# A 27-pass loop on five engines written out in a straight line

## The reference

```python
x = layernorm(x + attention(x))        # 16 query heads, 4 key/value heads of 64, rotary, ALiBi, out @ Wo
x = layernorm(x + cross_attention(x, ctx, cell))   # 16 heads of 16, windows of 64 keys and the 64 before,
                                       # causal, and only where cell[q] == cell[k]; layer norms before q, k, v, o
x = layernorm(x + ffn(x))              # bitlinear: ternary weights, activations rounded to 8 bits;
                                       # down(silu(gate(x)) * up(x)), inner width 1024
```

## Time and profile before

| | |
|---|---|
| median of 3 runs | 2457.42 us (2453.6 to 2459.31) |
| the profiled execution | 2455.23 us |
| its span, first to last instruction | 2453.3 us |
| mean granted TensorE clock | 0.978 |
| instructions | 61,410 |
| DMA | 72.93 MB, 30 GB/s over the span |

### The profile page before, as it was taken

One profiled execution on the slowest core, in us unless ns is written; L12 is line 12 of the kernel. 1 busy time (PEld: TensorE's weight loads), 2 busy tenths in 40 slices (PEclk: granted clock), 3 DMA queues, 4 the chain that ended last, 5 costly groups with the idle time before them and its releaser, 6 DMA issues. The chain is left out here.

```text
span 2453.3 us, 61410 instructions
## 1 busy us (share of the span) xinstructions
PE 2287.2 (93%) x17706; PEld 1662.5 (68%) x17706; DVE 1866.3 (76%) x8005; ACT 1568.6 (64%) x4577; POOL 1219.1 (50%) x1422
## 2 busy tenths in 40 slices
PE   5889999999999999999999999999999999999985
PEld 4666777776677776677766677676667776667652
DVE  4868887777787777787777787777787777787865
ACT  2567766667666667666667666667666667766651
POOL 3445554545554545454555454555455555454521
PEclk8999999999999999999999999999999999999996
DMA  4010110010110010011010011011011011010100
GB/s 156 15 37 20 32 34 19 24 33 24 31 33 25 19 33 27 28 33 32 11 33 27 28 33 32 11 33 30 26 31 32 11 33 30 26 31 24 29 10 13
DMA packets 84569, 72.93 MB, mean 30 GB/s; under 512 B 18336, under 2 KB 79136, under 8 KB 84384
## 3 DMA queue, kind: packets, MB, share of 16 engines
q1 hardware_dynamic: 84384, 71.19, 10.4%
HBM read 45.98 MB, written 8.39 MB: 22 GB/s over the span
## 5 line engine op out<-in xcount | busy, mean ns | idle before, releaser
L1151 POOL TENSOR_TENSOR prob<-prob,precs 128x512 f32<-128x512 f32 x512 | 528.7, 1045 | 414.9 <-DVE precs L809 410.5
L1066 ACT ACTIVATE prob<-prob,nmax 128x256 f32<-128x256 f32 x1024 | 508.3, 499 | 231.8 <-DVE nmax L802 231.8
L802 DVE CUSTOM_DVE_ANT_0 prob<-bank,alibi 128x256 f32<-128x256 f32 x1024 | 372.0, 419 | 148.3 <-PE bank L536 147.4
L1073 ACT COPY pT<-bank 128x512 f32<-128x512 f32 x512 | 298.9, 584 | 287.1 <-PE bank L441 281.2
L1089 ACT ACTIVATE px<-px,nmx 128x128 f32<-128x128 f32 x1024 | 316.0, 390 | 141.8 <-DVE nmx L894 139.8
L441 PE MATMUL bank<-ident,prob 128*128 128x128 f32 x2048 | 320.1, 280 | 8.2 <-ACT pT L1073 7.0
L1142 POOL TENSOR_TENSOR qtok<-qtok,by_sin 128x512 f32<-128x512 f32 x128 | 163.0, 1274 | 297.4 <-DVE by_sin L792 297.3
L441 PEld LDWEIGHTS bank<-ident,prob 128*128 128x128 f32 x2048 | 243.4, 143 | 96.1 <-issue 55.7
L536 PE MATMUL bank<-kk,qq 64*128 64x256 f32 x2048 | 291.3, 403 | 0.9 <-DVE nmax L802 0.9
L554 PE MATMUL bank<-pT,v_sb 128*64 128x256 f32 x2048 | 277.5, 392 | 7.7 <-ACT oT L1078 7.0
L894 DVE CUSTOM_DVE_ANT_0 px<-bank,mask 128x128 f32<-128x128 f32 x1024 | 230.4, 286 | 18.2 <-issue 4.8
(11 more groups left out here) (187 smaller groups left out, 4471.5 us busy)
## 6 DMA issues: line engine op xcount, KB each, us to landing
ctxt<-in_ctx SPq DMA_DIRECT2D x32, 256.0 KB, 2.7
xT<-in_xT SPq DMA_DIRECT2D x32, 256.0 KB, 3.0
cT<-in_ctxT SPq DMA_DIRECT2D x32, 256.0 KB, 2.6
xtok<-in_x SPq DMA_DIRECT2D x32, 256.0 KB, 3.0
kx<-kxT SPq DMA_DIRECT2D x256, 32.0 KB, 2.0
vs<-vx SPq DMA_DIRECT2D x64, 128.0 KB, 2.4
out_y<-y SPq DMA_DIRECT2D x32, 256.0 KB, 2.1
cellk<-in_cell SPq DMA_DIRECT2D x32, 64.0 KB, 2.9
```

Of the source, the lines that this page charges most:

```text
L802: v.tensor_tensor_reduce(out=prob[:, (2 * p + q) % SLOTS, c, :], in0=psum[SCORES[c]][:, q * L:(q + 1) * L], in1=alibi[:, p % 2, c, :], sca ...
L1066: nc.scalar.activation(prob[:, (2 * p + q) % SLOTS, c, :], prob[:, (2 * p + q) % SLOTS, c, :], ACT.Exp, bias=nmax[:, i:i + 1], scale=-1.0, ...
L1073: nc.scalar.copy(pT[:, p % 2, :, :, q * P:(q + 1) * P].rearrange("p c k n -> p (c k) n"), bank[:].rearrange("p (c n) -> p c n", c=4)).then ...
L1151: g.tensor_tensor(prob[:, n % SLOTS, :, :], prob[:, n % SLOTS, :, :], precs[:, 2 * n:2 * n + 2].unsqueeze(2).to_broadcast([P, 2, L]), ALU. ...
```

## The change

For each of the five engines the hardware loop is replaced by a loop of the program that writes the kernel, so that the 27 passes of BODY stand one after the other. The index is then a number, every wait compares with a constant, and every DMA has a constant address. HEAD, BODY, TAIL and `run` are as before. One of the five places, the others are alike (`pe`, `dve`, `act`, `pool` in place of `sp`):

```diff
             run(HEAD)
-            with sp.Fori(0, LAST - FILL) as j:
-                run(BODY, j + FILL)
+            for it in range(FILL, LAST):
+                run(BODY, it)
             run(TAIL)
```

More of the change, by code:

```diff
@@ L687, in _ @@
             run(HEAD)
-            with pe.Fori(0, LAST - FILL) as j:
-                run(BODY, j + FILL)
+            for it in range(FILL, LAST):
+                run(BODY, it)
             run(TAIL)
@@ L1029, in _ @@
             run(HEAD)
-            with dve.Fori(0, LAST - FILL) as j:
-                run(BODY, j + FILL)
+            for it in range(FILL, LAST):
+                run(BODY, it)
             run(TAIL)
@@ L1113, in _ @@
             run(HEAD)
-            with act.Fori(0, LAST - FILL) as j:
-                run(BODY, j + FILL)
+            for it in range(FILL, LAST):
+                run(BODY, it)
             run(TAIL)
@@ L1227, in _ @@
             run(HEAD)
-            with pool.Fori(0, LAST - FILL) as j:
-                run(BODY, j + FILL)
+            for it in range(FILL, LAST):
+                run(BODY, it)
             run(TAIL)
```

## The result

The changed kernel takes 2368.99 us (median of 4 runs, 2367.9 to 2370.26) against 2455.51 us for the kernel before in the same comparison. The ratio is 0.9649, 95% interval 0.9629 to 0.9668: 3.5% faster. The forecast was 2377 us, range 2362 to 2400.

The account below looks back on a forecast made before the run. TensorE was taken to bound the kernel, waiting for oT after VectorE's branch stalls. The wait's 58.8 us and the clock's 19.5, checked by 80.6 from whole passes, were taken as 80 saved, other terms nothing: 2377 us, range 2362 to 2400.

Parts of the forecast that it names:

- The bound and the place: TensorE waits for oT after VectorE's two stalls behind each taken branch: 58.8 us in 26 waits.
- The inference that the packets are VectorE's: Five 8 KB instruction blocks fetched again each loop pass were taken as VectorE's, which alone had an unexplained stall.
- The comparison of whole passes: 26 loop passes against the first, which has no branch before it: 1908.4 - 26 x 70.30 = 80.6 us saved.
- The other sum of the forecast: TensorE's wait for oT, 58.8 us, plus the clock's 19.5 us: together 78.3 us.
- The clock: TensorE's granted clock falls after the gap in about every second pass; 19.5 us, about 14 passes of 1.4 us.
- Rival (a): Gap goes, but the clock still falls or half a microsecond of wait returns each pass: about 2397 us, chance 0.08.
- The registers: Removing register operations in the 27 passes saves between nothing and 21 us; taken as nothing.
- Rival (b): Register work lay behind the last idle 0.77 us a pass; another 17 to 21 us go: about 2358, chance 0.04.
- TensorE's fetches: Straight code brings new 16 KB instruction blocks each pass, at most 1.6 us a block; taken as nothing.
- Rival (c): TensorE stalls at its instruction blocks: 2593 us at 1.6 us each, slower from 0.6 us a block; chance 0.05.
- Rival (d): No effect: VectorE's loop stays resident, packets are another engine's, the stall belongs to the step: 2457 us, chance 0.03.

Follow-up runs that it names:

- the kernel with 30: Kernel before, all loops kept, 30 semaphore increments added to VectorE ahead of HEAD: 2367.03 us, ratio 0.9628; timed again 2367.31 us.
- the kernel with 80: Kernel before, all loops kept, 80 semaphore increments added to VectorE ahead of HEAD: 2396.93 us, ratio 0.9755.
- 128: Kernel before, all loops kept, 128 semaphore increments (one whole block) added to VectorE ahead of HEAD: 2454.48 us, ratio 0.9983.

## Why the prediction was right, and where it was off

**The bound and the place.** The forecast named TensorE's wait for oT, made by VectorE's stalls behind the branch, and that was right. The wait went with VectorE's loop and with nothing else, in number (26, 8, 2 waits for 26, 8, 2 branches), and it went by the place of the code alone with 26 branches left.

**The inference that the packets are VectorE's.** Shown now: they go to 2.25 a pass when VectorE is written out, and to none when its loop is moved by 30 instructions.

**The comparison of whole passes.** 26 x (73.40 - 70.30) = 80.6 was forecast, 26 x (73.40 - 70.09) = 86.1 came. This is the term that was mis-sized: the first pass of before was a slightly too long model of a pass without a branch. In the changed kernel the same pass takes 69.97 us and the ones behind it 70.02 and 70.04. It isn't the registers: the first pass of the kernel with 30, with all of them, takes 69.96 us (293.10 to 363.06). Set beside that pass, the first of before loses 0.2 us at one place, the wait of TensorE at L554 for oT that the earlier trace rows shows, and 0.1 us after it. VectorE has this wait 5 us ahead of it, from 292 to 364 us:

```profile
DVE px L894 <- issue: 0.2, 1, 0.2
```

It is the small wait before the 264th instruction, at a block's edge. The first pass has it without any branch before it, so the comparison of a first pass with the others could not see it; the changed kernel and the one with 30 don't have it there. In the 26 passes it is the 4.6 us on VectorE and the 4.7 us at L554. The other sum of the forecast, 58.8 us for oT and 19.5 for the clock, left out the 4.7 us at L554 and the 3.2 us for hqT; it took the row of 10.8 us for pTx, which stayed, as the only other one. The rest of the 87.3 us lies before the second pass (it begins at 364.25 against 364.80 us) and behind the last.

**The clock.** It was taken as 19.5 us that go with the gap, about 14 passes of 1.4. That is borne out: in the 26 passes the trace of before has 13 stretches at the lower level (1.2 GHz) and that of the changed kernel none, and passes of two lengths (72.65, 74.50) turned into passes of one, 70.02 and 70.04. TensorE's matmul time fell by 24.1 us, rough by some 3. In the kernel with 80 the wait of 0.55 us left the clock at 1.00, so it was the long gap, not any wait at this place. Rival (a) did not come.

**The registers.** They were taken as nothing, with bounds of 0 and 21 us, and that was right. The kernel with all of them took 2367.31 us, the one with those of four engines 2367.45, the one with none 2367.12. Rival (b) did not come.

**TensorE's fetches.** They were taken as nothing, and that was right. Some 120 blocks (109 in 24 passes) cost less than can be measured; the three kernels differ by 0.33 us. Rival (c) wanted 0.6 us a block.

**Rival (d)** had a true part. VectorE's body can stay resident; it did not because of where it lay. The Trainium skill, in "Runtime: NRT & Kernel Launch", section "Instruction fetch mechanics", gives most engines 32 KiB of room, refilled in blocks of 16 KiB, the next one fetched while the current one runs. With the 8 KB that VectorE's packets carry here, this room would be four blocks, an estimate. The traces agree with a room of four: three blocks of body and one ahead stayed (30), four and one ahead were fetched anew, 5 packets a pass (before, and those with 80 and 128). The page's blocks of 16 KiB are not VectorE's in this case. That the room is four blocks is an inference from these placements, not measured by itself.

## What to carry to other kernels

Here the hardware loops were not costly by their registers or branches (2367.31 us with all of them). One was costly because VectorE's body, by the inference above with the block ahead of it, did not fit what the engine holds, and then once for each pass, on that engine alone. It showed as instruction packets inside the loop and as an "issue" wait a few instructions behind the branch. In another kernel, look for the engine that fetches before unrolling all of them: unroll that one, or shift its code. To price it beforehand, compare a first pass of the loop, which no branch precedes, with the others, taking the same instruction at both ends, and look for small waits that the first pass shares with them: this comparison can't see those (0.3 us a pass here).

## What the runs showed of the hardware that was not expected

- 30 increments of a semaphore that nothing waits for made the kernel 3.7% faster (2367.03 us), and 128 of them 0.2% (2454.48): the place of a loop over 8 KB blocks of code decided.
- A VectorE stall of 2.9 us (1.27 + 1.61) cost 3.31 us of every pass: 2.26 in TensorE's wait for oT, about 0.75 on average by the lower clock after it, and the remaining 0.3 in smaller waits.
- At the edge of a block further on in the body VectorE waited 0.2 us in each pass (before the 264th instruction in before, the 185th with 80 added). In one pass of the kernel with 80 this wait ends at 907.80 us, and no instruction packet starts between 880.42 and 908.42 us, so it isn't a packet that came late. What it is stays open. It doesn't show at every edge; in the straight code of VectorE (changed kernel) waits of kind "issue" are five single ones of 0.2 or 0.3 us, at different lines.
